# Low half of the second layer's weight: from GpSimd subtractions to a ScalarE pass and an accumulating transfer

## The chip, the cores and the metric

The kernel runs on one core of one Trainium2 chip. The metric is the device time of one execution, in microseconds (us). All work is in float32; the large matrix products use float32r operands (a rounded float32 that TensorE multiplies in one pass), each operand being split into a rounded high half and the remainder, the low half.

## The reference

The input x has shape (2, 2048, 512). It is layer-normalised to xn. Two branches start from xn:

- s: a selective state-space layer (a causal convolution of 4 taps, silu, projections to delta, B and C, and the recurrence h = exp(delta A) h + delta B x over 2048 time steps, 512 channels and 16 states), summed over the states with C, plus xn times D.
- a mixture of 8 experts with capacity 1024 tokens each, two experts per token. An expert is `gelu(disp @ fc1_w + fc1_b) @ fc2_w + fc2_b`, with a hidden width of 2048. Results are weighted by the gates and added per token; then silu gives g.

The output is x + s * g.

## The kernel before

`front` (the first 287 us) normalises, routes the tokens and prepares delta and u for the recurrence. `tail` (the last 100 us or so) combines the two branches. Between them, `main_loop` does two things at the same time: the experts' matrix products on TensorE and the recurrence on VectorE.

**The main loop's stages.** There are 8 chunks (one expert and one 512-step chunk of the recurrence each), and each chunk has 4 quarters of the hidden width, so 32 quarters in all. The code calls the quarter number within the chunk q, and `it` is the number from 0 to 31. A quarter's order on TensorE is written out by hand in 16 steps. Steps 0 to 7 are the first layer (`l1`): 12 matmuls of 512 columns each (three products, low x high, high x low, high x high, for 4 contraction tiles), written to one of four banks of the PSUM tensor `pm`. Steps 8 to 15 are the second layer (`l2`), again 12 matmuls each, into the same four banks. Behind each step's matmuls stand four transposes of finished recurrence rows (`turn_h`, L783 to L803). Steps 8, 9, 10 and 11 transpose a row whose scans number 2 and 3 of this quarter must be done (L788, L789). In a chunk's last quarter, `turn_x` also transposes the next expert's gathered tokens.

**Weights.** Each quarter needs two weights of 128 x 2048 values, w1 and w2 (1 MB each). Both go through the one buffer `raw`. SyncE loads it (`weights`, L714 to L719) once the semaphores `w_lo` and `w_hi` say that the previous content has been split. ScalarE writes the rounded high half (`split_w`, L879 to L884), w1's after the previous quarter's first layer, w2's between the gelus of steps 1 and 2 (L945, L946). GpSimd writes the low half as raw minus high (`low`, L1003 to L1010) in two operations of 128 x 1024 each. TensorE waits for `w_lo` ahead of both layers (L819, L838).

**ScalarE in a quarter.** Two gelus of 512 columns follow each first-layer step: one gives the high half `hh`, the other overwrites the bank in `pm` (L943, L944). After the four of g = 0 (steps 0 to 3) come the last two `exp` groups of the recurrence's decay factors (L947 to L949), which need another activation table, and then the gelus of g = 1 (steps 4 to 7). In a chunk's first quarter `bias_part` follows, which waits for the additions of the previous expert's rows to DRAM.

**VectorE in a quarter.** At even steps it does a pair of scans (`scans`, L1104 to L1113), 8 pairs in all; at each step a `sum_up` of one transposed row (L1082); at steps 0 to 7 `low_h` (L1088 to L1091), which subtracts `hh` from the bank in `pm` and so frees the bank (`h_free`), and at steps 8 to 15 `add_part` (L1099). In that order at step s: scans (if s is even), add_part, sum_up, low_h.

**GpSimd in a quarter.** The eight products `ub` (L1021), number i waiting for the pair of scans i - 2, with the four `low` parts between them: w1's first part ahead of all, its second after i = 0, w2's after i = 2 and i = 3. In a chunk's first quarter GpSimd also issues eight indirect transfers that add the previous expert's rows into DRAM (`add_tile`, L989), in the last quarter eight gathers (L978). All are on GpSimd's own DMA queue; all other transfers are on SyncE's.

Of the kernel before, what the change touches and what calls it, by code (L numbers as in the profile page):

```python
# [26 lines left out]
F32 = mybir.dt.float32  # L27
F32R = mybir.dt.float32r
I32 = mybir.dt.int32
ALU = mybir.AluOpType  # L30
ACT = mybir.ActivationFunctionType
# [3 lines left out]
P = 128  # L35
# [56 lines left out]
def apart(eng, sem):  # L92

    eng.sem_inc(sem, 1)
# [545 lines left out]
def main_loop(nc, a, dr, keep):  # L640

    with ExitStack() as ctx:
        sb, psum, sems = memory(nc, ctx)
        ident = sb("m_ident", [P, P])
        raw = sb("w_raw", [P, KT * QH])
        w1h, w1l = sb("w1h", [P, KT, QH], F32R), sb("w1l", [P, KT, QH], F32R)
        w2h, w2l = sb("w2h", [P, HT, D], F32R), sb("w2l", [P, HT, D], F32R)
        xTh, xTl = sb("xTh", [P, KT, CAP], F32R), sb("xTl", [P, KT, CAP], F32R)
        hh, hl = sb("hh", [P, 2, HT, 512], F32R), sb("hl", [P, 2, HT, 512], F32R)
        part = sb("part", [P, TILES, D])  # L650
# [10 lines left out]
        warm = sb("warm", [P, 2])  # L661
        pm = psum("pm", [P, 4, 512])
        pt = psum("pt", [P, 4, 512])
        s_ = sems("m_", """ident raw_in w_hi w_lo x_got0 x_got1 x_got2 x_got3 x_turned x_hi x_lo l1 gelu h_free l2
            acc_free exp h_turned summed bmul scan b_in0 b_in1 d_in u_in0 u_in1 s_out0 s_out1 s_out2 s_out3
            b2_in staged add_staged added0 added1 cleared biased carried act_at dve_at pool_at sp_at""")
        block = ctx.enter_context(nc.Block())
# [21 lines left out]
        def begins(e):  # L689
            return isinstance(e, int) and e == 0  # L690
# [177 lines left out]
        @block.scalar  # L868
        def _(act):
            act.sem_inc(s_["w_hi"], 1)  # L870
            act.sem_inc(s_["exp"], 1)

            act.wait_ge(s_["cleared"], 1)

            def split_x(e, t, bank):
                act.wait_ge(s_["x_turned"], TILES * e + t + 5)
                act.activation(xTh[:, :, t * P:(t + 1) * P], bank.rearrange("p (k s) -> p k s", k=KT), ACT.Copy).then_inc(s_["x_hi"], 1)

            def split_w(it, which):  # L879
                hi = w1h if which == 0 else w2h  # L880
                act.wait_ge(s_["raw_in"], 16 * (2 * it + which) + 16)

                act.wait_ge(s_["l1" if which == 0 else "l2"], 8 * it + 1)
                act.activation(hi[:].rearrange("p k f -> p (k f)"), raw[:], ACT.Copy).then_inc(s_["w_hi"], 1)  # L884

            def going(e):

                return keep["going"][:, ds(e, 1)]

            def chunk(e):  # L890
                def bias_part(t):

                    if t % 4 == 0:
                        act.wait_ge(s_[f"added{t // 4}"], 64 * e + 64)
                        act.wait_ge(s_["b2_in"], 16 * e + 16)
                        apart(act, s_["act_at"])
                    gate = keep["gate"][:].rearrange("p e j -> p (e j)")[:, ds(TILES * e + t, 1)]
                    act.activation(part[:, t, :], b2[:], ACT.Copy, scale=gate).then_inc(s_["biased"], 1)

                def quarter(it, q, first, last):  # L900
                    def exp(i):

                        m, h = i // 2, i % 2
                        if h == 0 and not (first and begins(e)):

                            act.wait_ge(s_["h_turned"], 16 * it + 4 * m - 12)
                            apart(act, s_["act_at"])
                            ends = abuf[:, m, :, CH - 1:CH]
                            if first:
                                act.activation(state[:, (N - NPQ + m) * KT:(N - NPQ + m + 1) * KT].unsqueeze(2), ends, ACT.Copy,  # L910
                                               scale=going(e)).then_inc(s_["carried"], 1)
                            else:
                                act.activation(state[:, ds(q * NPQ * KT + (m - NPQ) * KT, KT)].unsqueeze(2), ends, ACT.Copy,
                                               scale=going(e + 1)).then_inc(s_["carried"], 1)
                            act.wait_ge(s_["h_turned"], 16 * it + 4 * m - 12)
                            act.wait_ge(s_["carried"], 4 * it + m - 3)
                        for k in range(2):
                            kt = 2 * h + k
                            col = (q * NPQ + m) * KT + kt
                            op = act.activation(abuf[:, m, kt, :], delta[:, kt, :], ACT.Exp,  # L920
                                                scale=keep["neg_a"][:].rearrange("p n k -> p (n k)")[:, ds(col, 1)])
                        op.then_inc(s_["exp"], 1)


                    if not (first and begins(e)):
                        split_w(it, 0)
                    tokens = first and not begins(e)
                    lag = 2 if tokens else 0
                    for i in range(LATE + lag):
                        if tokens:  # L930
                            split_x(e, i, pt[:, (1 + 2 * i) % 4, :])
                        if first and i == lag:
                            act.wait_ge(s_["d_in"], 16 * e + 16)
                        if i >= lag:
                            exp(i - lag)

                    act.activation(warm[:, 1:2], warm[:, 0:1], ACT.Gelu)
                    for g in range(2):
                        for j in range(HT):
                            act.wait_ge(s_["l1"], 8 * it + 4 * g + j + 2)  # L940
                            apart(act, s_["act_at"])
                            bias = keep["b1"][:, ds(4 * it + j, 1)]
                            act.activation(hh[:, g, j, :], pm[:, j, :], ACT.Gelu, bias=bias)  # L943
                            act.activation(pm[:, j, :], pm[:, j, :], ACT.Gelu, bias=bias).then_inc(s_["gelu"], 1)  # L944
                            if g == 0 and j == 1:  # L945
                                split_w(it, 1)  # L946
                        if g == 0:  # L947
                            for i in range(LATE, 8):
                                exp(i)  # L949
                    if first:  # L950
                        for t in range(TILES):
                            bias_part(t)

                quarters(e, act, quarter)


            for t in range(TILES):
                split_x(0, t, pm[:, t % 4, :])
                if t == 3:
                    split_w(0, 0)  # L960
            chunks(act, chunk)

        @block.gpsimd
        def _(pool):
            pool.sem_inc(s_["w_lo"], 1)
            pool.sem_inc(s_["bmul"], 4)

            def stage_rows(e):
# [21 lines left out]
                                        compute_op=ALU.add).then_inc(s_[f"added{t // 4}"], 16)  # L990


            LOWS = {0: (0, 1), 2: (1, 0), 3: (1, 1)}
            ADDS = {1: (0, 1), 2: (2, 3), 3: (4,), 4: (5, 6), 5: (7,)}
            GATHERS = {1: (0, 1), 2: (2,), 3: (3,), 5: (4, 5), 6: (6,), 7: (7,)}

# [3 lines left out]

            def chunk(e):
                def quarter(it, q, first, last):
                    def low(which, part):  # L1003
                        hi, lo = ((w1h, w1l), (w2h, w2l))[which]
                        pool.wait_ge(s_["w_hi"], 2 * it + which + 2)
                        w = raw[:].rearrange("p (k f) -> p k f", k=KT)
                        k = slice(KT // 2 * part, KT // 2 * (part + 1))
                        op = pool.tensor_tensor(lo[:, k], w[:, k], hi[:, k].bitcast(F32), ALU.subtract)  # L1008
                        if part == 1:
                            op.then_inc(s_["w_lo"], 1)  # L1010

                    low(0, 0)
                    for i in range(8):
                        m, h = i // 2, i % 2
                        if first and i < 2:
# [3 lines left out]
                            pool.wait_ge(s_[f"b_in{m % 2}"], 16 * (2 * it + m // 2) + 16)  # L1019
                        pool.wait_ge(s_["scan"], 8 * it + i + 1)  # L1020
                        pool.tensor_tensor(ub[:, h], u[:, 2 * h:2 * h + 2, :], brow[:, m % 2:m % 2 + 1, :].to_broadcast([P, 2, CH]), ALU.mult).then_inc(s_["bmul"], 1)  # L1021
                        if i in LOWS:
                            low(*LOWS[i])
                        if first:
                            if i == 1:
                                stage_adds(e)
# [108 lines left out]
def tail(nc, a, dr, keep, out):  # L1135

    with ExitStack() as ctx:
        sb, psum, sems = memory(nc, ctx)
        TPP = 2
        RING = 12  # L1140
        PC, NP = TPP * P, NT // TPP
        d_row, shift = sb("t_D", [P, D]), sb("t_shift", [P, NT])
        s, y, x, o = (sb(f"t_{n}", [P, RING, TPP, D]) for n in "syxo")
        parts = " ".join(f"xs{p} y{p} out{p}" for p in range(NP))
        s_ = sems("t_", f"consts {parts} shift silu xn skip whole gated sum")
        block = ctx.enter_context(nc.Block())

# [1 line left out]
        def _(sp):  # L1149
# [8 lines left out]

            def store(p):
                sp.wait_ge(s_["sum"], p + 1)  # L1160
                sp.dma_start(out[p].rearrange("(j p) d -> p j d", p=P), o[:, p % RING]).then_inc(s_[f"out{p}"], 16)

            for p in range(RING):
                load(p)
            for p in range(NP):
                store(p)
                if p + RING < NP:
                    load(p + RING)
            for p in range(NP):
                sp.wait_ge(s_[f"out{p}"], 16)  # L1170

        @block.scalar
        def _(act):
# [121 lines left out]
```

## Time and profile before

| | |
|---|---|
| median of 3 runs | 2094.13 us (2093.86 to 2094.44) |
| the profiled execution | 2093.87 us, of which 2092.1 us are the span |
| TensorE matmul busy | 1879.3 us, 90% of the span |
| VectorE busy | 1837.1 us, 88% |
| GpSimd busy | 1333.8 us, 64% |
| ScalarE busy | 1228.4 us, 59% |
| DMA moved | 244.78 MB |
| main loop, first matmul of quarter 0 to first of quarter 31 | 311.5 to 1937.8 us |

The span is the time from the first to the last profiled instruction; the time of an execution is 1.8 us longer. PE is TensorE, PEld its loading of weights, DVE VectorE, ACT ScalarE, POOL GpSimd, SP SyncE; a "q" behind the name is the engine's sequencer, which issues transfers. Matmuls overlap one another in the records, so their mean duration is longer than their spacing. "pm<-xTh,w1l" means that the instruction writes pm and reads xTh and w1l.

### The profile page before, as it was taken

Reading aid. Unit: us, or ns where it says so; the run is one execution under the profiler, and the core shown is the slowest. Engines: PE = TensorE matmul, PEld = TensorE weight load, DVE = VectorE, ACT = ScalarE, POOL = GpSimd, SP = SyncE. Lnnn points to the kernel's source line nnn. Section 1 sums busy time; section 2 is a strip of 40 time slices with the busy share of each in tenths; the row PEclk is TensorE's granted clock in tenths of the full one; section 3 lists DMA queues with packets and bytes.
Section 4 is the critical chain, followed back from the end, with each engine's and each line's share of the span. In section 5 each row is a group of like instructions: output and inputs, shape, how many; then the busy total and the mean of one; then the engine's idle time right before and its main releaser. Section 6 shows DMA issues by size and latency. Waiting matters only on the chain. (4 is left out here: it accounts for less than half of the span.)

```text
span 2092.1 us, 30245 instructions
## 1 busy us (share of the span) xinstructions
PE 1879.3 (90%) x9032; PEld 1464.4 (70%) x9032; DVE 1837.1 (88%) x1959; ACT 1228.4 (59%) x1799; POOL 1333.8 (64%) x645
## 2 busy tenths in 40 slices
PE   6599929999999999999999999999999999999900
PEld 3233217888788888888888788888887888888800
DVE  6556648989998999899989998999899989998869
ACT  3267747566656665666556655666566656665443
POOL 1167758567866786678667866786678667865600
PEclk9799959999999999999999999999999999999955
DMA  8713454213421342135223512351145114511299
GB/s 285 263 42 103 102 199 97 85 65 131 107 85 65 130 109 82 65 125 118 74 72 123 121 64 74 130 122 61 68 139 122 61 63 144 121 61 60 57 306 381
DMA packets 88547, 244.78 MB, mean 117 GB/s; under 512 B 13168, under 2 KB 14192, under 8 KB 77168
## 3 DMA queue, kind: packets, MB, share of 16 engines
q1 hardware_dynamic: 70640, 207.30, 28.4%
q0 software_dynamic: 17536, 35.73, 9.3%
q8 instruction: 66, 1.08, 0.2%
q14 instruction: 49, 0.40, 0.1%
q10 hardware_dynamic: 256, 0.26, 0.1%
HBM read 171.56 MB, written 71.70 MB: 116 GB/s over the span
## 5 line engine op out<-in xcount | busy, mean ns | idle before, releaser
L1111 DVE TENSOR_TENSOR_SCAN a_sb<-a_sb,state,ub_sb 128x512 f32<-128x512 f32 x512 | 901.6, 1801 | 9.8 <-issue 6.3
L1021 POOL TENSOR_TENSOR ub_sb<-u_sb,brow_sb 128x1024 f32<-128x1024 f32 x256 | 632.1, 2469 | 388.7 <-DVE a_sb L1111 388.3
L772 PE MATMUL pm<-xTh,w1l 128*128 128x512 f32 x1024 | 423.9, 414 | 16.1 <-POOL w1l L1008 7.2
L772 PE MATMUL pm<-w2h,hl 128*128 128x512 f32 x1024 | 422.9, 413 | 0.0
L774 PE MATMUL pm<-xTh,w1h 128*128 128x512 f32 x1024 | 402.3, 393 | 0.0
L774 PE MATMUL pm<-w2h,hh 128*128 128x512 f32 x1024 | 401.8, 392 | 0.0
L773 PE MATMUL pm<-xTl,w1h 128*128 128x512 f32 x1024 | 398.6, 389 | 0.0
L773 PE MATMUL pm<-w2l,hh 128*128 128x512 f32 x1024 | 398.5, 389 | 0.0
L1082 DVE SCALAR_TENSOR_TENSOR s_acc<-pt,ct_keep,s_acc 128x512 f32<-128x512 f32 x480 | 352.8, 736 | 19.8 <-PE pt L802 19.0
L920 ACT ACTIVATE a_sb<-delta_sb,neg_a_keep 128x512 f32<-128x512 f32 x512 | 330.2, 713 | 6.7
L802 PE MATMUL pt<-m_ident,a_sb 128*128 128x128 f32 x2048 | 306.1, 272 | 3.8 <-DVE a_sb L1111 3.8
L802 PEld LDWEIGHTS pt<-m_ident,a_sb 128*128 128x128 f32 x2048 | 252.0, 139 | 71.6 <-issue 5.8
L943 ACT ACTIVATE hh<-pm,b_keep 128x512 fp32r<-128x512 f32 x256 | 175.9, 687 | 164.2 <-PE pm L774 160.2
L772 PEld LDWEIGHTS pm<-xTh,w1l 128*128 128x128 f32 x1024 | 193.3, 189 | 50.0 <-issue 14.5
L1008 POOL TENSOR_TENSOR w2l<-w_raw,w2h 128x1024 fp32r<-128x1024 f32 x64 | 194.7, 3042 | 47.0 <-ACT w2h L884 46.8
L774 PEld LDWEIGHTS pm<-xTh,w1h 128*128 128x128 f32 x1024 | 192.5, 188 | 43.8
L774 PEld LDWEIGHTS pm<-w2h,hh 128*128 128x128 f32 x1024 | 192.1, 188 | 43.3
L773 PEld LDWEIGHTS pm<-xTl,w1h 128*128 128x128 f32 x1024 | 193.9, 189 | 32.5
L773 PEld LDWEIGHTS pm<-w2l,hh 128*128 128x128 f32 x1024 | 193.5, 189 | 32.5
L1099 DVE SCALAR_TENSOR_TENSOR part<-pm,gate_keep,part 128x512 f32<-128x512 f32 x256 | 187.3, 732 | 32.6 <-PE pm L774 32.6
L772 PEld LDWEIGHTS pm<-w2h,hl 128*128 128x128 f32 x1024 | 192.9, 188 | 30.7
L1091 DVE TENSOR_TENSOR hl<-pm,hh 128x512 fp32r<-128x512 f32 x256 | 174.2, 681 | 39.3 <-ACT pm L944 35.6
(135 smaller groups left out, 2004.7 us busy)
## 6 DMA issues: line engine op xcount, KB each, us to landing
w_raw<-in_w SPq DMA_DIRECT2D x64, 1024.0 KB, 4.8
brow_sb<-b_chunks SPq DMA_DIRECT2D x128, 256.0 KB, 3.2
moe_rows<-zeros_sb SPq DMA_DIRECT2D x5, 2048.0 KB, 16.7
xin_sb<-in_x SPq DMA_DIRECT2D x8, 1024.0 KB, 6.3
xn_rows<-xn_sb SPq DMA_DIRECT2D x8, 1024.0 KB, 8.5
delta_chunks<-ln_sb SPq DMA_DIRECT2D x8, 1024.0 KB, 5.8
u_chunks<-u_now_sb SPq DMA_DIRECT2D x16, 512.0 KB, 5.7
delta_sb<-delta_chunks SPq DMA_DIRECT2D x8, 1024.0 KB, 7.9
```

Of the source, the lines that this page charges most:

```text
L772: pe.matmul(out, sl, mh, start=start, stop=False)
L773: pe.matmul(out, sh, ml, start=False, stop=False)
L774: return pe.matmul(out, sh, mh, start=False, stop=stop)
L802: mm = pe.transpose(pt[:, bank(s, last), kt * P:(kt + 1) * P], abuf[:, m, kt, tb * P:(tb + 1) * P], ident[:])
L920: op = act.activation(abuf[:, m, kt, :], delta[:, kt, :], ACT.Exp, scale=keep["neg_a"][:].rearrange("p n k -> p (n k)")[:, ds(col, 1)])
L943: act.activation(hh[:, g, j, :], pm[:, j, :], ACT.Gelu, bias=bias)
L1008: op = pool.tensor_tensor(lo[:, k], w[:, k], hi[:, k].bitcast(F32), ALU.subtract)
L1021: pool.tensor_tensor(ub[:, h], u[:, 2 * h:2 * h + 2, :], brow[:, m % 2:m % 2 + 1, :].to_broadcast([P, 2, CH]), ALU.mult).then_inc(s_["bmul ...
L1082: dve.scalar_tensor_tensor(out=acc, in0=h, scalar=c, in1=acc, op0=ALU.mult, op1=ALU.add).then_inc(s_["summed"], 1)
L1091: dve.tensor_tensor(hl[:, g, j, :], pm[:, j, :], hh[:, g, j, :].bitcast(F32), ALU.subtract).then_inc(s_["h_free"], 1)
L1099: dve.scalar_tensor_tensor(out=part[:, t, :], in0=pm[:, t % 4, :], scalar=gate, in1=part[:, t, :], op0=ALU.mult, op1=ALU.add).then_inc(s_[ ...
L1111: op = dve.tensor_tensor_scan(abuf[:, m, 2 * h + k, :], abuf[:, m, 2 * h + k, :], ub[:, h, k, :], state[:, ds(col, 1)], ALU.mult, ALU.add)
```

## The change

GpSimd no longer computes the low half of w2. ScalarE writes the negative of the rounded raw into `w2l` (an extra pass ahead of the high half); GpSimd then issues one direct transfer from `w2l` to `raw` with an adding operation, so that `raw` becomes raw minus high; when it has landed, ScalarE copies `raw` into `w2l`, rounding it (`finish_w2`, after the last two exp groups of the quarter). This last copy, instead of GpSimd's second part, tells TensorE and SyncE through `w_lo`. The w1 parts on GpSimd stay, at the places where they were. In the tail, the last 12 output transfers share one semaphore.

```diff
@@ scalar
             act.sem_inc(s_["w_hi"], 1)
+            act.sem_inc(s_["w_lo"], 1)
             act.sem_inc(s_["exp"], 1)
...
                 act.wait_ge(s_["l1" if which == 0 else "l2"], 8 * it + 1)
+                if which == 1:
+                    act.activation(w2l[:].rearrange("p k f -> p (k f)"), raw[:], ACT.Copy, scale=-1.0).then_inc(s_["w2_neg"], 1)
                 act.activation(hi[:].rearrange("p k f -> p (k f)"), raw[:], ACT.Copy).then_inc(s_["w_hi"], 1)
+
+            def finish_w2(it):
+                act.wait_ge(s_["w2_rest"], 16 * it + 16)
+                apart(act, s_["act_at"])
+                act.activation(w2l[:].rearrange("p k f -> p (k f)"), raw[:], ACT.Copy).then_inc(s_["w_lo"], 1)
...
                         if g == 0:
                             for i in range(LATE, 8):
                                 exp(i)
+                            finish_w2(it)
@@ gpsimd
-            pool.sem_inc(s_["w_lo"], 1)
             pool.sem_inc(s_["bmul"], 4)
...
-            LOWS = {0: (0, 1), 2: (1, 0), 3: (1, 1)}
...
-                    def low(which, part):
-                        hi, lo = ((w1h, w1l), (w2h, w2l))[which]
-                        pool.wait_ge(s_["w_hi"], 2 * it + which + 2)
+                    def low(part):
+                        pool.wait_ge(s_["w_hi"], 2 * it + 2)
                         w = raw[:].rearrange("p (k f) -> p k f", k=KT)
                         k = slice(KT // 2 * part, KT // 2 * (part + 1))
-                        op = pool.tensor_tensor(lo[:, k], w[:, k], hi[:, k].bitcast(F32), ALU.subtract)
+                        op = pool.tensor_tensor(w1l[:, k], w[:, k], w1h[:, k].bitcast(F32), ALU.subtract)
                         if part == 1:
                             op.then_inc(s_["w_lo"], 1)
 
-                    low(0, 0)
+                    def rest():
+                        pool.wait_ge(s_["w2_neg"], it + 1)
+                        pool.wait_ge(s_["w_hi"], 2 * it + 3)
+                        apart(pool, s_["pool_at"])
+                        pool.dma_start(raw[:], w2l[:].rearrange("p k f -> p (k f)").bitcast(F32), accum_op=ALU.add).then_inc(s_["w2_rest"], 16)
+
+                    low(0)
                     for i in range(8):
...
-                        if i in LOWS:
-                            low(*LOWS[i])
+                        if i == 0:
+                            low(1)
+                        if i == 2:
+                            rest()
```

## Rows read from the trace of the kernel before

**Rows 1.** The page, busy time, share and instructions of two engines.
```profile
PE 1879.3 (90%) x9032; PEld 1464.4 (70%) x9032; DVE 1837.1 (88%) x1959; ACT 1228.4 (59%) x1799; POOL 1333.8 (64%) x645
```

**Rows 2.** Timeline, quarter 21 on TensorE: start us, us, instruction [idle before <-releaser].
```profile
1415.66 0.49 PE L772 MATMUL pm<-xTh,w1l 128*128 128x512 f32 x1 [0.69 <-POOL w1l L1008]
...
1441.18 0.47 PE L772 MATMUL pm<-w2h,hl 128*128 128x512 f32 x1
...
1444.02 0.60 PE L802 MATMUL pt<-m_ident,a_sb 128*128 128x128 f32 x4
...
1466.68 0.47 PE L772 MATMUL pm<-xTh,w1l 128*128 128x512 f32 x1
```

**Rows 3.** Windows: us, busy by engine (x instructions), PEclk, DMA share, GB/s.
```profile
1415.66:1466.68 51.02, 51.02 (x257) 42.31 (x257) 49.89 (x52) 29.62 (x42) 30.59 (x13) 1.00 0.22 75
1435.70:1438.20 2.50, 2.50 (x15) 2.08 (x14) 2.50 (x4) 2.21 (x5) 1.29 (x1) 1.00 0.91 308
1399.40:1401.90 2.50, 2.50 (x14) 2.04 (x13) 2.50 (x4) 0.00 (x0) 1.91 (x1) 1.00 0.84 105
```

**Rows 4.** Waits over the whole span: who <- for whom, us in total, times, longest.
```profile
PE pm L772 <- POOL w1l L1008: 7.2, 8, 2.3
...
PE pm L772 <- DVE part L1099: 4.1, 4, 1.1
...
PE pt L802 <- DVE a_sb L1111: 3.8, 7, 0.7
```

**Rows 5.** Groups by line: name, shapes, count | busy us, mean ns | idle before.
```profile
L1008 POOL TENSOR_TENSOR w2l<-w_raw,w2h 128x1024 fp32r<-128x1024 f32 x64 | 194.7, 3042 | 47.0 <-ACT w2h L884 46.8
```

**Rows 6.** Timeline, quarter 21 on ScalarE.
```profile
1423.23 1.92 ACT L884 ACTIVATE w2h<-w_raw 128x2048 fp32r<-128x2048 f32 x1
1425.26 0.69 ACT L943 ACTIVATE hh<-pm,b_keep 128x512 fp32r<-128x512 f32 x1
...
1428.45 0.69 ACT L943 ACTIVATE hh<-pm,b_keep 128x512 fp32r<-128x512 f32 x1 [1.95 <-PE pm L774]
...
1433.96 1.28 ACT L943 ACT_TABLE_LOAD   x1
...
1435.84 0.65 ACT L944 ACTIVATE pm<-pm,b_keep 128x512 f32<-128x512 f32 x1
...
1442.28 1.92 ACT L884 ACTIVATE w1h<-w_raw 128x2048 fp32r<-128x2048 f32 x1
```

**Rows 7.** Timeline, quarter 21 on GpSimd.
```profile
1425.23 3.41 POOL L1008 TENSOR_TENSOR w2l<-w_raw,w2h 128x1024 fp32r<-128x1024 f32 x1
1429.80 2.40 POOL L1021 TENSOR_TENSOR ub_sb<-u_sb,brow_sb 128x1024 f32<-128x1024 f32 x1 [1.16 <-DVE a_sb L1111]
```

**Rows 8.** Timeline, quarter 21 on VectorE.
```profile
1432.14 4.69 DVE L1111 TENSOR_TENSOR_SCAN a_sb<-a_sb,state,ub_sb 128x512 f32<-128x512 f32 x2
...
1437.40 0.67 DVE L1091 TENSOR_TENSOR hl<-pm,hh 128x512 fp32r<-128x512 f32 x1
...
1439.25 2.45 DVE L1111 TENSOR_TENSOR_SCAN a_sb<-a_sb,state,ub_sb 128x512 f32<-128x512 f32 x2
```

**Rows 9.** DMA issues: line, count, KB each, median us from issue to landing.
```profile
w_raw<-in_w SPq DMA_DIRECT2D x64, 1024.0 KB, 4.8
...
moe_rows<-part,add_now POOLq DMA_INDIRECT x72, 5.7
```

**Rows 10.** GpSimd's own transfers, issue time in ns, min/median/max.
```profile
L989 POOL DMA_INDIRECT moe_rows<-part,add_now x72: 1551/1939/2348, 316.6 to 1990.3; - x72
...
L978 POOL DMA_INDIRECT got<-xn_rows,row_now x64: 947/987/2022, 288.4 to 1770.5; - x64
```

**Rows 11.** Timeline, quarter 20 (a chunk's first): ScalarE, SyncE and TensorE.
```profile
1370.43 1.92 ACT L884 ACTIVATE w2h<-w_raw 128x2048 fp32r<-128x2048 f32 x1
...
1377.55 1.58 SPq L730 DMA_DIRECT2D s_rows<-s_acc  x2
...
1392.00 0.65 PE L802 MATMUL pt<-m_ident,a_sb 128*128 128x128 f32 x4 [0.63 <-DVE a_sb L1111]
```

More of the change, by code:

```diff
@@ L663, in main_loop @@
         pt = psum("pt", [P, 4, 512])
-        s_ = sems("m_", """ident raw_in w_hi w_lo x_got0 x_got1 x_got2 x_got3 x_turned x_hi x_lo l1 gelu h_free l2
+        s_ = sems("m_", """ident raw_in w_hi w2_neg w2_rest w_lo x_got0 x_got1 x_got2 x_got3 x_turned x_hi x_lo l1 gelu h_free l2
             acc_free exp h_turned summed bmul scan b_in0 b_in1 d_in u_in0 u_in1 s_out0 s_out1 s_out2 s_out3
@@ L1143, in tail @@
         s, y, x, o = (sb(f"t_{n}", [P, RING, TPP, D]) for n in "syxo")
-        parts = " ".join(f"xs{p} y{p} out{p}" for p in range(NP))
+        parts = " ".join(f"xs{p} y{p}" for p in range(NP)) + " out0 out1 out2 out3 outs"
         s_ = sems("t_", f"consts {parts} shift silu xn skip whole gated sum")
@@ L1160, in store @@
                 sp.wait_ge(s_["sum"], p + 1)
-                sp.dma_start(out[p].rearrange("(j p) d -> p j d", p=P), o[:, p % RING]).then_inc(s_[f"out{p}"], 16)
+                sp.dma_start(out[p].rearrange("(j p) d -> p j d", p=P), o[:, p % RING]).then_inc(s_[f"out{p}" if p < NP - RING else "outs"], 16)
             for p in range(RING):
@@ L1168, in _ @@
                     load(p + RING)
-            for p in range(NP):
+            for p in range(NP - RING):
                 sp.wait_ge(s_[f"out{p}"], 16)
+            sp.wait_ge(s_["outs"], 16 * RING)
         @block.scalar
```

## The prediction

> **What bounds the kernel now.** I read the page's busy times first, then TensorE's timeline, then the waits, and last the other engines inside one quarter. The page gives TensorE 90% and VectorE 88% of the span [rows 1], which decides nothing. TensorE's timeline decides. Quarter 21 begins at 1415.66 and the next one at 1466.68, and its second layer begins at 1441.18 [rows 2]: 25.5 us for each layer's eight steps, so 3.19 us a step. Within that quarter TensorE is busy for all of its 51.02 us at a granted clock of 1.00, the level of 2.4 GHz [rows 3]. The same halves of 25.5 us stand in all quarters in which TensorE waits for nothing. In the whole span its waits for others in the main loop are 7.2 us for w1's low half, 4.1 us for `add_part` and 3.8 us for scans [rows 4]. So the main loop is TensorE's, and an engine that gets faster can give back about 15 us at most. An engine that comes late costs what it is late, once in each quarter, because TensorE takes its steps in order and never has time to catch up.
>
> VectorE is second. It is busy for 49.9 of the quarter's 51.0 us [rows 3], but part of that is waiting inside its records: a pair of scans takes 2.45 us beside an idle GpSimd and 4.69 us beside GpSimd's products and w2's low half [rows 8].
>
> **The change, part by part.**
>
> *Removed from GpSimd:* two operations a quarter with a mean of 3.04 us, 194.7 us in all [rows 5]. GpSimd is not the bound. What comes free is VectorE's time: up to 4.69 - 2.45 = 2.2 us for each of the two, 4.5 us a quarter. It is worth only what TensorE waits for VectorE or for GpSimd behind VectorE, the 15 us above. The waits at a chunk's last quarter (4.1 us) I take as gone; the others I treat below.
>
> *Added to ScalarE ahead of w2's high half:* one more pass of 128 x 2048, 1.92 us [rows 6]. The high half ended at 1425.15 and will end at about 1427.0. The next gelu moves from 1425.26 to 1427.1 and the one behind it stays at 1428.45, since before it ScalarE stood 1.95 us idle for TensorE [rows 6]. So this pass costs nothing on that side; if that cover were gone it would cost 1.9 us. What it delays is the start of the low half, from 1425.23 [rows 7] to 1427.15.
>
> *Added to GpSimd:* one direct transfer. GpSimd waits for both passes until 1427.15, then issues. Behind it stands the product that began at 1429.80 [rows 7]. An issue of 1 to 2 us is over by then, so its cost to GpSimd is nothing; in a chunk's first quarter two adding transfers stand behind it too, 2 us later than the end of w2's high half before, but there the removed operation had held them back by 3.2 us. Gathers in the last quarter have a longer lead still.
>
> *Added to ScalarE behind the exps:* a wait for the landing and a third pass of 1.92 us. Behind this wait stand the four gelus of steps 4 to 7, and behind them VectorE. This is the path that sets the end. Let F be the time at which the third pass begins. Before, the gelu table was loaded at 1433.96, and the second gelu of step 4 ended 2.53 us later (1435.84 + 0.65) [rows 6]. Now it ends at F + 1.92 + 2.53 = F + 4.45. `low_h` of step 4 follows at F + 4.55. The pair of scans behind it (number 3) began 1439.25 - 1437.40 = 1.85 us after that `low_h` and took 2.45 us [rows 8], so it ends at F + 8.85. TensorE's transposes behind step 8, at 1444.02 [rows 2], need those scans. So F may be 1435.1 at the latest without a stall. The exps are over at 1433.96, and the transfer, issued at 1427.15, must land by 1434.95: it has 7.8 us. Each microsecond beyond is a microsecond of TensorE, in each of the 32 quarters. The waits for w2l itself (at 1441.18) and for the bank of step 4 come later on this scale (F = 1439.2 and 1435.9) and don't decide. `raw` also comes free later, at F + 1.9, 1437.0 for an F at the limit. Its next load takes 4.8 us [rows 9], to 1441.8, and w1's high half, the first to read it, began at 1442.28 [rows 6] and hurries nobody for the rest of the layer, so that is hidden.
>
> *How long the transfer takes* no row shows; it has three terms. Issue: a gather of 256 KB takes GpSimd 0.95 us at least, an adding transfer 1.55 us [rows 10]; I take 1.3 us. Fixed time: the 1 MB load lands after 4.8 us [rows 9]. In the stretch 1435.7 to 1438.2 it runs at 308 GB/s at a share of 0.91, so 338 GB/s at full share, or 3.1 us for 1 MB [rows 3]; its rest is 1.7 us with the issue of 0.33 us, and I take 1.5 us. Data: the plain rate gives 3.1 us. The adding transfer alone runs at 105 GB/s at a share of 0.84, or 125 GB/s, which gives 8.4 us for 1 MB [rows 3]. It works in pieces of 2 KB on DRAM, where the new one has rows of 8 KB in SBUF. I take 6.2 us, twice the plain time, since each byte needs a second read. The bounds are 1.0 + 1.5 + 3.1 = 5.6 us and 1.9 + 1.7 + 8.4 = 12.0 us; my value is 1.3 + 1.5 + 6.2 = 9.0 us, near the middle of them; an adding transfer of a quarter of the bytes lands after 5.7 us [rows 9], and 9.0 us leaves it 3.3 us for the other three quarters. So, with 0.1 us to ScalarE's start, F is 1436.25 and the stall is 1.2 us.
>
> The Trainium skill, DMA: Bandwidth & Descriptors, section "Anatomy of one DMA — SWDGE (gpsimd) path", fits a GpSimd-issued transfer by 2.0 us plus bytes at 436 GB/s, and Collectives: The Full Stack, section "The bandwidth ceiling: the fold count and why AG ≠ RS ≠ AR", says that an add needs two source reads and so halves the rate. By both, an estimate is 2.0 + 2 x 2.4 = 6.8 us, inside the 7.8 us, and the sum would have no stall at all. No row here shows such a transfer; the rows give a slower plain rate and an issue on top.
>
> **The sum.** Quarters 2 and 3 of each chunk (16): 16 x 1.2 = 19 us. The first quarters (8): there w2's high half starts at 1370.43, the new transfer would be issued at 1374.35, and two stores of 256 KB are issued from 1377.55 on, while it runs [rows 11]; 512 KB at 338 GB/s are 1.6 us, of which I count 1.2 us. TensorE already waited 0.63 us for the same scans there [rows 11], so 1.2 + 1.2 - 0.6 = 1.8 us each, 14 us. The last quarters (8): 8 x 1.2 less the 4.1 us that VectorE's relief gives back, 6 us. The wait for w1's low half at a chunk's second quarter I leave, because the additions to DRAM that it hangs on come behind the same late scans. The tail's semaphores cost nothing: the waits before the last one are over while the last store is under way. Together 39 us. The profiled execution took 2093.87 us (span 2092.1 and 1.8 around it), 0.3 us under the median; 2093.9 + 39 = 2133 us.
>
> **The rivals.**
>
> *The transfer is in time (faster).* If it lands within 7.8 us, F falls at the latest to 1435.1 and nothing of TensorE's path moves. Then VectorE's relief of 4.5 us a quarter decides: 4.1 and 3.8 us of waits go, and with scans earlier the additions' last transfer and so the 7.2 us for w1's low half. That is 15 us, 2079 us. For it speaks the large rows of 8 KB and that both ends lie in SBUF; the short fixed part of the load says it too. Against it, the adding rows show that adding costs more than twice the plain time. It decides from 1 MB of data in 5.0 us or less (7.8 less 2.8). Chance 0.24. The Trainium skill's two rules above, DMA: Bandwidth & Descriptors and Collectives: The Full Stack, would make this the likely case.
>
> *Just in time (no change).* A landing near 8.0 us: 0.2 to 0.4 us of stall in 32 quarters, about 10 us, stands against the same relief. 2090 to 2098 us. Chance 0.13.
>
> *The adding rate of the rows holds (much slower).* Data at 125 GB/s makes the landing 10.6 to 12 us. At 10.6 us the stall is 2.8 us: 45 + 27 + 18 = 90 us, 2184 us; at 12.0 us it is 4.2 us: 67 + 38 + 30 = 135 us, 2229 us. Here VectorE's queue behind `low_h` is the place, as above. For it speaks that this is the only adding rate in the trace; against it, that those transfers are small and go to DRAM. Chance 0.15.
>
> The forecast, a landing of 8.2 to 10.5 us, has 0.48.
>
> **Range and chances.** The range goes from the faster rival's 2079 us to the 2184 us of a 10.6 us landing; faster relief and the full small-piece rate stay outside. The forecast's own range is 2105 to 2180 us. About 0.2% (4 us) is what a measurement of this kernel can tell from no change. Faster 0.24, same 0.13, slower 0.63.
>
> **What the profile of the changed kernel would show.** The copy into w2l on ScalarE stands behind the exps with idle time ended by the transfer into w_raw; its landing is about 9 us after issue. Halves of quarters: the first layer still 25.5 us, the second 26.7 us, with the added time in front of the transposes of step 8, released by scans. Pairs of scans of 2.45 us at w2's place. GpSimd's busy time falls by about 195 us less 32 issues. The prediction is wrong if the landing is under 7.8 us, if TensorE's added wait stands elsewhere (at w2l or at the banks of pm), or if matmuls' spacing changes.

## The result and the profile after

The changed kernel takes 2107.27 us (median of 4 runs, 2104.40 to 2111.01) against 2094.28 us: a ratio of 1.0058, with a 95% interval of 1.0043 to 1.0073. Forecast were 2133 us, slower. The direction holds, the size doesn't: 13.0 us were lost where 39 us were forecast, and the time lies at the lower edge of the forecast's own range (2105 to 2180 us). The profiled execution took 2105.57 us with a span of 2103.7 us.

The page of the changed kernel, the engines' shares, and three of its groups: VectorE's scans, `low_h`, and TensorE's transposes:

```profile
PE 1880.7 (89%) x9032; PEld 1462.3 (70%) x9032; DVE 1735.9 (83%) x1959; ACT 1338.4 (64%) x1863; POOL 1175.9 (56%) x613
...
L1125 DVE TENSOR_TENSOR_SCAN a_sb<-a_sb,state,ub_sb 128x512 f32<-128x512 f32 x512 | 803.0, 1608 | 8.0 <-issue 6.0
...
L1105 DVE TENSOR_TENSOR hl<-pm,hh 128x512 fp32r<-128x512 f32 x256 | 174.6, 682 | 201.7 <-ACT pm L952 198.0
...
L802 PE MATMUL pt<-m_ident,a_sb 128*128 128x128 f32 x2048 | 307.1, 273 | 11.2 <-DVE a_sb L1125 11.0
```

TensorE does the same work (1880.7 us busy against 1879.3 in [rows 1]). VectorE is busy for 101 us less and GpSimd for 158 us less (forecast were 195 us less 32 issues, about 153), and yet the kernel is slower. VectorE now stands 198 us idle for ScalarE's gelus, and TensorE's transposes wait 11.0 us for scans where they waited 3.8 us [rows 4].

The waits of the changed kernel over the span (who <- for whom, us in total, times, longest):

```profile
ACT w2l L892 <- DMA w_raw<-w2l: 51.1, 32, 2.9
...
POOL ub_sb L1033 <- DMA brow_sb<-b_chunks: 21.4, 7, 4.2
...
PE pt L802 <- DVE a_sb L1125: 11.0, 17, 1.3
...
PE pm L772 <- POOL w1l L1014: 3.4, 5, 0.7
...
PE pm L772 <- DVE hl L1105: 3.1, 3, 1.8
```

ScalarE waits for the transfer in all 32 quarters, 1.6 us on average, and TensorE pays only where the third pass begins later than its path allows. Quarter 22, the third of its chunk, shows the forecast chain. It begins at 1472.59. On GpSimd, ScalarE, VectorE and TensorE its timeline reads:

```profile
1484.43 0.89 POOL L1022 DMA_DIRECT2D w_raw<-w2l  x1 [3.19 <-ACT w2h L887]
```
```profile
1491.91 1.92 ACT L892 ACTIVATE w2l<-w_raw 128x2048 fp32r<-128x2048 f32 x1 [1.06 <-DMA w_raw<-w2l]
1493.85 1.28 ACT L951 ACT_TABLE_LOAD   x1
...
1495.73 0.65 ACT L952 ACTIVATE pm<-pm,b_keep 128x512 f32<-128x512 f32 x1
```
```profile
1496.41 0.69 DVE L1105 TENSOR_TENSOR hl<-pm,hh 128x512 fp32r<-128x512 f32 x1 [5.75 <-ACT pm L952]
...
1498.28 2.45 DVE L1125 TENSOR_TENSOR_SCAN a_sb<-a_sb,state,ub_sb 128x512 f32<-128x512 f32 x2
```
```profile
1500.91 0.60 PE L802 MATMUL pt<-m_ident,a_sb 128*128 128x128 f32 x4
```

From issue to the third pass are 7.48 us. The scans end at 1500.73 and the transposes of step 8 begin at 1500.91, 28.32 us into the quarter, where they stood 28.36 us into quarter 21 before [rows 2]. So here the transfer is just in time. One quarter later, a chunk's last, two gathers were issued ahead of the transfer on the same DMA queue and one behind it. From issue to the third pass are 8.22 us in place of 7.48, ScalarE's wait is 1.94 us in place of 1.06, and TensorE waits at the same transposes:

```profile
1552.62 0.65 PE L802 MATMUL pt<-m_ident,a_sb 128*128 128x128 f32 x4 [0.56 <-DVE a_sb L1125]
```

The last quarter of the last chunk, which issues no gathers, is back at 7.53 us from issue to the third pass.

The length of a quarter, from the first matmul to that of the next quarter, taken from TensorE's timelines (means over chunks 1 to 7, and 1 to 6 for the last quarters), with the main loop from the first matmul of quarter 0 to the start of the last transpose:

| quarter of its chunk | before | changed |
|---|---|---|
| first | 52.77 us | 53.02 us |
| second | 51.01 | 51.25 |
| third | 50.99 | 51.02 |
| last | 55.49 | 56.14 |
| main loop | 1679.0 | 1688.3 |
| from its end to the span's end | 101.6 | 105.4 |

The main loop lost 9.3 us, the stretch behind it 3.8 us, and the stretch ahead gave 1.5 us. Behind the loop the late scans show too. In the last quarter one product of GpSimd waited 8.30 us for scans; the eight additions to DRAM at the end are issued one behind another after the last product, and the last one leaves 2.8 us after the last transpose (1998.32), where before it left 0.2 us ahead of it (1990.27 against 1990.50). Timeline of GpSimd, changed kernel:

```profile
1973.80 2.41 POOL L1033 TENSOR_TENSOR ub_sb<-u_sb,brow_sb 128x1024 f32<-128x1024 f32 x1 [8.30 <-DVE a_sb L1125]
...
2001.09 1.55 POOL L997 DMA_INDIRECT moe_rows<-part,add_now  x1 [0.30 <-issue]
```

The runs below bear this out: in every one the span ends 101.4 to 102.9 us after the start of this last addition, while the time from the last transpose to the end goes from 101.1 to 105.7 us. They also show that the transfer isn't the whole of it (see "No transfer, and a plain one").

### The profile page after: what moved, and what is told of

It is laid out like the page before. It is cut to its first block and busy times, and to the rows that moved or that the text cites. A ratio compares the mean times of both kernels' runs of the same rounds, so it can differ in the third digit from the quotient of the medians.

```text
span 2103.7 us, 30391 instructions
## 1 busy us (share of the span) xinstructions
PE 1880.7 (89%) x9032; PEld 1462.3 (70%) x9032; DVE 1735.9 (83%) x1959; ACT 1338.4 (64%) x1863; POOL 1175.9 (56%) x613
## 5 line engine op out<-in xcount | busy, mean ns | idle before, releaser
L1125 DVE TENSOR_TENSOR_SCAN a_sb<-a_sb,state,ub_sb 128x512 f32<-128x512 f32 x512 | 803.0, 1608 | 8.0 <-issue 6.0
L921 ACT ACTIVATE state<-a_sb,going_keep 128x4 f32 (+1 forms) x96 | 29.3, 305 | 259.0 <-PE pt L802 259.0
```

The costliest lines, as they stand in the source:

```text
L1125: op = dve.tensor_tensor_scan(abuf[:, m, 2 * h + k, :], abuf[:, m, 2 * h + k, :], ub[:, h, k, :], state[:, ds(col, 1)], ALU.mult, ALU.add)
```

## The experiments

The time ahead of the main loop differs between executions (its first matmul comes at 310 to 329 us, whatever the kernel), so beside each ratio stands the main loop of the profiled execution, defined as above. Theory: the transfer's landing has a deadline, because the gelus of steps 4 to 7, `low_h` and a pair of scans stand behind ScalarE's wait; what is late beyond it is paid by TensorE. Rivals: ScalarE's extra passes, the transfer's traffic, or the tail's shared semaphore.

### Third pass later

```diff
                             if g == 0 and j == 1:
                                 split_w(it, 1)
+                            if g == 1 and j == 1:
+                                finish_w2(it)
...
-                            finish_w2(it)
```

> The third ScalarE pass (finish_w2) stands behind the gelus of steps 4 and 5 instead of ahead of them. Theory (the landing has a deadline, because gelus, low_h and scans stand behind the wait): the pass now begins about 22 us into the quarter, when the transfer has long landed, the wait for scans at step 8 (11.0 us in all) and for low_h (3.1 us) go, and the main loop is at or below the time of the kernel before: 2082 to 2094 us. Rival (ScalarE's extra passes or the transfer's traffic cost the time wherever they stand): 2105 to 2110 us. Second rival (w_raw comes free too late for the next load): about 2110 us with ScalarE waiting for w_raw.

Measured: 1.0034 of the kernel before (1.0016 to 1.0052), main loop 1680.9 us. The third pass begins at about 21.8 us into the quarter and waits for nothing; the waits for scans at step 8 and for `low_h` are gone, and third and last quarters are at 50.99 and 55.36 us. So the deadline's part is right, and most of the main loop's loss is gone (1688.3 to 1680.9 us; 1679.0 before). Behind the loop are 102.1 us, near the 101.6 before. These two explain 2.4 us of the 7 us that the ratio stands for; the rest was not placed. The forecast of 2082 to 2094 us was missed: first quarters are still 53.02 us. What TensorE waits for is now at the start of a chunk's second quarter:

```profile
1433.49 0.49 PE L772 MATMUL pm<-xTh,w1l 128*128 128x512 f32 x1 [2.33 <-POOL w1l L1015]
```

and GpSimd's timeline in the first quarter before it, which began at 1379.93, shows where that starts:

```profile
1391.79 0.97 POOL L1023 DMA_DIRECT2D w_raw<-w2l  x1 [2.21 <-ACT w2h L887]
1393.06 1.61 POOL L998 DMA_INDIRECT moe_rows<-part,add_now  x1 [0.31 <-issue]
...
1404.50 2.70 POOL L1034 TENSOR_TENSOR ub_sb<-u_sb,brow_sb 128x1024 f32<-128x1024 f32 x1 [3.10 <-DMA brow_sb<-b_chunks]
1407.36 1.57 POOL L998 DMA_INDIRECT moe_rows<-part,add_now  x1 [0.15 <-issue]
```

A product waits for a row of B (256 KB), which was issued while the adding transfer, two additions and stores of s had the DMA engines. Behind that product stand the next additions, behind their landing `bias_part` on ScalarE, behind it the high half of the next w1, and behind that its low half.

### No transfer, and a plain one

```diff
-                        pool.dma_start(raw[:], w2l[:].rearrange("p k f -> p (k f)").bitcast(F32), accum_op=ALU.add).then_inc(s_["w2_rest"], 16)
+                        pool.sem_inc(s_["w2_rest"], 16)
```

> The accumulating transfer is left out, so w2l gets the rounded weight and not the remainder; GpSimd only sends the semaphore. All three ScalarE passes stay. Theory: the third pass starts as soon as the exps are over, 18.3 us into the quarter, 1.1 us ahead of the deadline; no stall at step 8; 2080 to 2094 us. Rival (the passes on ScalarE cost it): 2105 to 2110 us, unchanged.

Measured: 0.9931 (0.9909 to 0.9954), main loop 1663.4 us, 15.5 us under the kernel before. In the main loop ScalarE's three passes cost nothing, then. First quarters fall from 52.77 to 51.01 us; over all eight, the first chunk's among them, that is 14.9 us. Last quarters are at 55.41 us (55.49 before).

Behind the loop the passes do cost something. With nothing to wait for, the stretch from the last transpose to the end is still 103.5 us against 101.6, and the last addition to DRAM still leaves 1.6 us after the last transpose (at 1992.64):

```profile
1994.29 1.55 POOL L997 DMA_INDIRECT moe_rows<-part,add_now  x1 [0.30 <-issue]
```

In the two runs with the third pass behind the gelus of step 5 it leaves 0.3 us ahead of it, as in the kernel before, with the adding transfer (102.1 us to the end) and with a plain one (101.1 us). So about half of the 3.8 us is the place of the third pass, ahead of gelus and scans. The rest comes with the adding transfer, in a way that was not followed up: with the early split, where the pass waits for nothing in the last chunk's last quarter, the stretch is 104.4 us.

```diff
-                        pool.dma_start(raw[:], w2l[:].rearrange("p k f -> p (k f)").bitcast(F32), accum_op=ALU.add).then_inc(s_["w2_rest"], 16)
+                        pool.dma_start(raw[:], w2l[:].rearrange("p k f -> p (k f)").bitcast(F32)).then_inc(s_["w2_rest"], 16)
```

> The transfer overwrites raw instead of adding to it, so the low half of w2 is the negative high half. Same bytes, same queue, no second read. Theory: it lands after 4.5 to 5.5 us instead of about 7.4, before the exps are over; the third pass waits for nothing; 2080 to 2094 us, as without a transfer. Rival (fixed time and issue on GpSimd are the bulk of the 7.4 us): the wait of the third pass stays within 0.5 us of the changed kernel's 1.1 us in a chunk's third quarter, 2105 us.

Measured: 0.9941 (0.9917 to 0.9965), main loop 1665.6 us. The issue and the landing, from the view of that line:

```profile
L1022 POOL DMA_DIRECT2D w_raw<-w2l x32: 558/592/620, 333.7 to 1944.6; - x32
...
  ACT w2l L892: 1.1, 1
...
DMA to landing us min/median/max: 4.4/4.6/6.2
```

Against the adding transfer's issue:

```profile
L1022 POOL DMA_DIRECT2D w_raw<-w2l x32: 881/934/1001, 323.9 to 1957.4; - x32
```

So adding costs 0.34 us more of issue. From issue to landing it costs 2.8 us more in third quarters: 4.6 us here, and 7.4 us in the changed kernel, where the third pass begins 7.48 us after the issue. 4.6 us is far inside the slack, and ScalarE waits once in 32 quarters. Behind the loop are 103.6 us, as without a transfer. The rival that the fixed time is the bulk falls.

### Transfer issued later

```diff
-                        if i == 2:
+                        if i == 3:
                             rest()
```

> GpSimd issues the transfer behind product 3 instead of product 2, some 3.4 us later. Theory: each quarter has no slack left, so each pays nearly the whole delay: 32 x 3.3 = 105 us, 2200 to 2215 us, the stall split between the first second-layer matmul (bank of step 4) and the transposes of step 8. Rival (the transfer's landing is not what decides): under 2130 us.

Measured: 1.0597 (1.0567 to 1.0626), main loop 1806.3 us: 118 us over the changed kernel, where 105 were expected. The stall stands where it was expected:

```profile
ACT w2l L892 <- DMA w_raw<-w2l: 164.1, 32, 8.8
...
PE pm L772 <- DVE hl L1105: 94.0, 32, 6.6
```

Second and third quarters are 2.5 and 3.3 us longer than in the changed kernel, though the issue moved by only 1.6 us at most of them (to 13.46 us into a third quarter from 11.85). The third pass moved by 2.9 us there (22.2 from 19.3), so the transfer itself took 1.3 us longer. What it met is a row of B, which waits for product 3 as the transfer now does: in the third quarter that begins at 1565.6 us SyncE issued it at 1579.37, 0.3 us after the transfer (1579.08). No run separates the two. First quarters are 6.1 us longer: there the issue moved by 4 us or so, behind additions to DRAM. The expectation had the whole delay at the issue and the same delay everywhere; the sum came out near by offsetting parts. What the run shows is that there is no slack left to take a delay in any quarter.

### Split started earlier

```diff
-                            if g == 0 and j == 1:
+                            if g == 0 and j == 0:
                                 split_w(it, 1)
```

> The two passes that start w2's split stand behind the gelus of step 0 instead of step 1, all else as in the changed kernel. Theory (deadline): the transfer is issued about 2.2 us earlier, 9.6 us into the quarter, and lands at 16.9 to 17.5 us, ahead of the end of the exps at 18.3; the waits at step 8 go; main loop 10 to 15 us shorter than before, as without a transfer, less if the additions of a chunk's first quarter still suffer from the transfer's traffic; 0.993 to 1.000 of the kernel before. Rival (the gelus of step 1 are now late by 2.6 us and hold TensorE up at step 5): 1.01 and more.

Measured: 0.9974 (0.9960 to 0.9987), main loop 1672.2 us, faster than both kernels, but 6.8 us under the kernel before and not the 10 to 15 us expected. The issue came at 10.3 us in third quarters and about 9.6 us in second ones, since the second pass ended later than I had reckoned in some. The landing in the list of transfers:

```profile
w_raw<-w2l POOLq DMA_DIRECT2D x32, 1024.0 KB, 7.3
```

This median mixes 6.9 us in third quarters, 7.6 us in last ones and about 8 us in first ones. In third quarters it landed 17.2 us in, before the exps ended, and ScalarE began the third pass at 18.16 us without a wait. Second to last quarters are at 51.00, 50.99 and 55.46 us. First quarters are at 52.04 us, better than before but not at the 51.0 us of the run with no transfer: TensorE still waits 3.5 us in them for w1's low half and 1.7 us for scans, in all. The rival, that the gelus of step 1 hold TensorE up at step 5, falls.

### Later pass with a plain transfer

> As the run with the third pass behind step 5's gelus, but the transfer overwrites raw instead of adding to it (w2's low half is then the negative high half). Nothing waits for the landing in either, so the two differ only in how long the DMA engines are taken. Theory (in a chunk's first quarter the broadcast of B and the additions to DRAM queue behind the adding transfer, so bias_part, w1's split and w1's low half come late for the second quarter): first quarters fall from 53.5 us to 51 to 52 us, main loop 8 to 14 us shorter. Rival (the late third pass itself delays first quarters): they stay at 53 us and more.

Its edit is the later third pass and the plain transfer together. Measured: 0.9926 (0.9909 to 0.9943), main loop 1664.9 us, 16.0 us under the run with the same order and the adding transfer. First quarters fell from 53.02 to 51.04 us and the 12.4 us of waiting for w1's low half to 0.7 us. In neither run does the third pass wait for the landing, so it is how long the transfer occupies the DMA engines and its queue that costs first quarters their gain.

### The tail alone, and the changed kernel again

> The kernel before with the tail's shared semaphore alone. Both theories: no difference, 0.999 to 1.001. If the tail's part of the change cost the 3.8 us that the changed kernel shows behind its last matmul, 1.002.

Measured: 0.9999 (0.9988 to 1.0009), 101.4 us from the last transpose to the end against 101.6. The tail's shared semaphore does nothing.

> The changed kernel once more, beside the others on the same chip, for the spread of its time: 1.004 to 1.008 of the kernel before, with 7.4 to 7.6 us from issue to the third pass in a chunk's third quarter.

Measured: 1.0073 (1.0056 to 1.0090), main loop 1689.5 us against 1688.3 in the first profile. From issue to the third pass are 7.5 us in third quarters, as before.

### Row of B ahead of the stores

```diff
+                    load_b(it, q, 2)
                     if first and not begins(e):
                         for tb in range(TPC):
                             store_s(tb)
-                    for m in range(2, NPQ):
-                        load_b(it, q, m)
+                    load_b(it, q, 3)
```

with the early split (the first run below), and alone on the kernel before (the second).

> The early-split version, and in a chunk's first quarter SyncE issues the third broadcast of B ahead of the four stores of s instead of behind them, so some 5 us sooner and ahead of the adding transfer. Theory (what is left in first quarters is this broadcast waiting on busy DMA engines, 25.0 us of GpSimd's waiting in 7 places, then late products, scans, additions and w1's low half): GpSimd's wait for brow_sb falls under 5 us, first quarters from 51.2 to 52.6 us to about 51.0, main loop 5 to 8 us under the early-split version; 0.992 to 0.996 of the kernel before. Rival (the additions themselves are slowed by the transfer): unchanged, 0.997.

Measured: 0.9932 (0.9911 to 0.9953), main loop 1664.5 us, the fastest version with the whole computation. First quarters are at 51.00 us. GpSimd's products no longer wait for a row of B, and of TensorE's waits in the main loop only these are left (the 4.3 us stand ahead of its first matmul, all the others at the ends of last quarters):

```profile
PE pm L772 <- issue: 4.9, 2, 4.3
...
PE pm L772 <- DVE part L1113: 3.7, 4, 1.1
```

> The kernel before with that reordering of SyncE's transfers alone. Its broadcast waited for nothing there (0.9 us in the whole span), so no difference: 0.999 to 1.001. If the reordering helps by itself, under 0.998.

Measured: 1.0006 (0.9990 to 1.0022). Alone the reordering is worth nothing; with the adding transfer and the early split it gave 7.6 us of main loop (1672.2 to 1664.5).

## Why the prediction was right and wrong

**What bounds the kernel** was right. TensorE has no time to catch up, and its instructions are the same in both kernels (1880.7 and 1879.3 us busy over the span). In the main loop it is idle for 15.7 us before and 21.6 us after. The other 3.4 us of the 9.3 stand inside the records, which for the same instructions are busy that much longer; where was not read.

**The place of the stall** was right in the main: the third pass behind the landing, then `low_h` of step 4, the third pair of scans, and the transposes behind step 8. Three first quarters stalled at the bank of step 4 too (3.1 us in all), which the prediction had put later. The forecast limit of F, 1435.1 in quarter 21, is 19.4 us into a quarter. In the changed kernel the third pass begins 19.3 us into third quarters, with no stall to speak of (51.02 us), and 20.1 us into last ones, where TensorE waits 0.5 us at step 8 and the quarter is 0.65 us longer (56.14 against 55.49). In the run with the later issue it begins 22.2 us in, and third quarters are 3.3 us longer, 0.5 us more than the limit says; most of TensorE's waiting then stands at the bank of step 4.

**The step that failed is the length of the transfer.** The prediction put "1.3 + 1.5 + 6.2 = 9.0 us" for issue, fixed time and data. In third quarters of the changed kernel it took 7.4 us: 0.93 us of issue, 5.1 us of data, and 1.4 us for the rest. The data term is the one that was mis-sized most. A window of the changed kernel in the middle of such a transfer answers to those in [rows 3]:

```profile
1486.00:1489.00 3.00, 3.00 (x17) 2.49 (x16) 2.88 (x4) 2.81 (x6) 1.75 (x1) 1.00 0.99 205
```

205 GB/s at a share of 0.99 are 207 GB/s, or 5.1 us for 1 MB, where 6.2 us were assumed and 8.4 us stood as the bound from the additions in pieces of 2 KB. The 6.2 us were twice the plain time at 338 GB/s, and that rate was misread: the window 1435.70 to 1438.20 lay over the start of the load, when its first pieces were still slow. Split in two, the same stretch of the kernel before shows it, and below it stands the plain transfer inside SBUF:

```profile
1435.70:1437.00 1.30, 1.30 (x8) 1.04 (x7) 1.30 (x2) 1.30 (x4) 0.09 (x1) 1.00 0.80 189
1437.00:1438.50 1.50, 1.50 (x10) 1.29 (x9) 1.50 (x3) 1.21 (x3) 1.50 (x1) 1.00 1.03 437
```
```profile
1479.30:1481.30 2.00, 2.00 (x10) 1.63 (x9) 1.88 (x3) 1.82 (x3) 1.42 (x1) 1.00 0.99 397
```

Once under way the load from DRAM ran at 424 GB/s at full share and the plain transfer at 401, so 2.5 to 2.6 us for 1 MB each; twice that is the 5.1 us seen. Two readings for each byte fit, then, and the error was in the rate that was doubled. Reckoned the prediction's way with 2.5 us, the load's rest grows to 2.0 us without its issue, and the sum is 1.3 + 2.0 + 5.0 = 8.3 us: still 0.9 us too much, in issue and rest.

With 7.4 us in place of 9.0, the stall of 1.2 us in second and third quarters is 0 by the prediction's own sum; 19 of the 39 us go with it, and its own sign of being wrong, a landing under 7.8 us, came true. The slack was smaller as well. GpSimd issued the transfer 11.85 us into the quarter where 11.5 were forecast, so it was 7.5 us and not 7.8, and the transfer made it by 0.1 us. An error of 1.6 us in the transfer is more than the whole forecast stall, so that a size could not be forecast from it.

Part of the 7.4 us is company. With the early split the same transfer landed after 6.9 us in third quarters. In the changed kernel SyncE issues a row of B while it runs (at 1487.98 in quarter 22), with the early split only as it ends. That this row is what makes the 0.5 us is an inference; no run moved it alone.

The Trainium skill's two rules (DMA: Bandwidth & Descriptors, "Anatomy of one DMA — SWDGE (gpsimd) path", and Collectives: The Full Stack, "The bandwidth ceiling: the fold count and why AG ≠ RS ≠ AR", which says it of ReduceScatter) gave 6.8 us by their estimate. Measured were 6.9 us for the adding transfer with little beside it, 7.4 us in the changed kernel, and 4.6 us for the plain one, where the fit gives 4.4 us; they were nearer than my sum from rows. But "no stall at all" does not follow, since last quarters run 0.65 us over.

By part of the sum, forecast and measured (sums over the chunks):

| part | forecast | measured |
|---|---|---|
| first quarters | 14 us | 1.8 us |
| second and third | 19 | 3.0 |
| last | 6 | 4.5 |
| behind the loop | 0 | 3.8 |
| ahead of the loop | 0 | -1.5 |

That is 39 us against 11.6, the difference of the profiled spans.

**The relief** was right in total, by luck, and wrong in its place. Forecast were 15 us at most if the transfer cost nothing; without it the main loop is 15.5 us shorter. Of these I had booked 4.1 us at the ends of last quarters. There next to nothing changed (55.41 us without a transfer, 55.49 before): TensorE's wait for `add_part` is 3.6 us even then. 14.9 us are in first quarters: the 7.2 us of waits for w1's low half, an item that the prediction "leaves", the 3.8 us of waits for scans, and 3.8 us that no wait in the trace before shows. It also explains why first quarters ended so near to before: 0.25 us longer in place of the 1.8 us forecast, because the stall and the traffic took nearly all of a relief that I had not counted there.

**The rivals.** The changed kernel lies between two of them: the transfer is "just in time" in third quarters and late in last ones. "No change" was priced at 10 us of stall against 10 us of relief; measured were 0.65 us in each last quarter, 0.8 to 1.1 us in two second ones, 3.8 us behind the loop, and a relief that the queues ate. The stretch behind the loop had no term in the sum but the tail's semaphores. The much slower case did not come: the small-piece rate does not hold for rows of 8 KB inside SBUF.

## What to carry to other kernels

Where a wait is added on an engine with a fixed order, write down by when it must be over and follow what stands behind it to the bounding engine; that limit came out right to about 0.1 us here, while the estimate of the transfer was 1.6 us too long, more than the stall that it gave. Take a transfer's rate from a stretch in which it is already under way. Follow a late engine past the loop as well: its last work can be what the next stage waits for. A large transfer has two prices, its own landing and what it does to small ones issued while it runs. Start it early, and issue the small ones that are needed soon ahead of it: here that turned 1.0058 into 0.9932.

## What was not expected

A direct adding transfer of 1 MB within SBUF lands 6.9 us after issue with little beside it and 7.4 us beside a row of B, a plain one after 4.6 us. The third row of B in a first quarter, a broadcast of 256 KB, landed 4.9 to 6.0 us after its issue before (chunks 1 to 7) and 8.5 to 10.7 us in the changed kernel, when the adding transfer, two additions and stores were on the engines; GpSimd waited up to 4.2 us for it. GpSimd's issue of the adding form takes 0.93 us and of the plain form 0.59 us for the same rows.
